# First attention: masks of the scores moved from TensorE products to GpSimd, key blocks weighed in pairs

## What is computed

```python
bias = slopes[None, :, None, None] * pos_diff[None, None, :, :]
causal = jnp.where(jnp.triu(jnp.ones((s, s), bool), 1), -jnp.inf, 0.0)[None, None]
s0 = jnp.einsum('bhqd,bhkd->bhqk', q0, k0) * scale - bias + causal
s1 = jnp.einsum('bhqd,bhkd->bhqk', q1, k1) * scale - bias + causal
w0 = jax.nn.softmax(s0, axis=-1)
w1 = jax.nn.softmax(s1, axis=-1)
...
diff_weights = w0 - lamb * w1
heads = jnp.einsum('bhqk,bhkd->bhqd', diff_weights, v).transpose(0, 2, 1, 3)
```

## Time and profile before

| | us |
|---|---|
| three runs, lowest / median / highest | 4068.45 / 4080.18 / 4084.04 |
| span of the profiled execution | 4082.1 |
| busy in it: PE / DVE / ACT / POOL | 3563.8 / 2450.6 / 2022.2 / 1270.3 |

### The profile page before, as it was taken

How to read it: one execution, slowest core, us unless ns; L and a number is a source line. 1 busy time by engine, 2 the same in 40 slices (tenths; PEclk the granted TensorE clock), 3 DMA queues, 4 the chain that set the end, 5 groups by cost and what they waited for, 6 DMA issues and landing times. The chain is left out here.

```text
span 4082.1 us, 86911 instructions
## 1 busy us (share of the span) xinstructions
PE 3563.8 (87%) x28212; PEld 2170.8 (53%) x28212; DVE 2450.6 (60%) x5697; ACT 2022.2 (50%) x3970; POOL 1270.3 (31%) x1812
## 2 busy tenths in 40 slices
PE   5799999969996698995999986788986699999997
PEld 2344444436774222222677762368974366666665
DVE  5677777741113688885677776517646566666654
ACT  5466666643335477773233334333344565656562
POOL 0111111100001011110677762605565344444440
PEclk9799999979997799996999997887788799999999
DMA  4322222200001311110666631130005233333330
GB/s 125 83 56 55 57 53 59 48 1 16 11 6 42 79 45 43 41 36 12 174 159 157 160 94 60 36 101 3 3 18 71 86 118 114 118 114 114 118 105 21
DMA packets 198052, 287.18 MB, mean 70 GB/s; under 512 B 40922, under 2 KB 155297, under 8 KB 197461
## 3 DMA queue, kind: packets, MB, share of 16 engines
q1 hardware_dynamic: 193688, 275.28, 24.2%
q0 software_dynamic: 4096, 8.40, 1.4%
HBM read 232.38 MB, written 35.84 MB: 66 GB/s over the span
## 5 line engine op out<-in xcount | busy, mean ns | idle before, releaser
L709 ACT ACTIVATE att_E<-att_pX,att_gs 128x512 f32<-128x512 f32 (+3 forms) x1024 | 723.5, 740 | 421.2 <-PE att_pX L643 176.5
L742 DVE TENSOR_REDUCE att_mx<-att_pS 128x1 f32<-128x512 f32 (+4 forms) x960 | 732.4, 787 | 202.7 <-PE att_pS L617 170.5
L1833 POOL TENSOR_TENSOR att_E<-att_E,att_rz 128x128 f32<-128x128 f32 (+3 forms) x512 | 358.3, 721 | 430.9 <-DVE att_rz L2041 430.9
L637 PE MATMUL att_pX<-arr_qs,arr_ks 75*128 75x512 bf16 (+4 forms) x1536 | 427.3, 334 | 27.6 <-ACT att_E L709 12.6
L612 PE MATMUL att_pS<-arr_ks,arr_qs 72*128 72x512 bf16 (+4 forms) x1536 | 410.3, 339 | 42.9 <-DVE att_pO L732 12.6
L1573 POOL TENSOR_TENSOR pairs_h<-pairs_m,pairs_r 128x512 f32<-128x512 f32 x272 | 346.4, 1274 | 192.0 <-DVE pairs_m L1636 182.9
L574 POOL CAST att_mp<-att_m 16x128 bf16<-16x128 f32 x288 | 81.2, 282 | 932.9 <-DVE att_m L753 907.7
L1597 PEld LDWEIGHTS pairs_po<-pairs_a,pairs_h 128*128 128x128 f32 x2176 | 286.4, 192 | 130.2 <-issue 129.4
L654 PE MATMUL att_pO<-att_E,att_vs 128*9 128x512 f32 (+3 forms) x3072 | 328.6, 500 | 1.3 <-ACT att_E L709 1.3
L1618 ACT ACTIVATE pairs_r<-pairs_ph 128x512 f32<-128x512 f32 x272 | 162.6, 598 | 327.6 <-PE pairs_ph L1589 327.6
L1972 ACT ACTIVATE att_E<-att_S,att_nm 128x128 f32<-128x128 f32 (+3 forms) x512 | 282.1, 556 | 38.6 <-DVE att_nm L2035 38.5
(11 more groups left out here) (411 smaller groups left out, 6551.5 us busy)
## 6 DMA issues: line engine op xcount, KB each, us to landing
pairs_c<-weights SPq DMA_DIRECT2D x272, 256.0 KB, 3.9
att_bias<-in_bias_dram SPq DMA_DIRECT2D x64, 896.0 KB, 4.5
parts<-proj_part SPq DMA_DIRECT2D x144, 128.0 KB, 2.3
att_xb<-xnT SPq DMA_DIRECT2D x64, 256.0 KB, 2.7
arr_qs<-parts SPq DMA_DIRECT2D x192, 64.0 KB
arr_ks<-parts SPq DMA_DIRECT2D x192, 64.0 KB
att_w<-in_w3a_dram SPq DMA_DIRECT2D x64, 192.0 KB, 2.4
arr_qs<-parts SPq DMA_DIRECT2D x96, 96.0 KB
```

What stands on the lines that cost most here:

```text
L637: ins = nc.tensor.matmul(dst[:, n], ks[:, g % NB, x, kt * P:(kt + 1) * P], qs[:, g % NB, x, q0(kt):], start=(apart or n == 0), stop=not ca ...
L709: nc.scalar.activation(E[:, kt % 2, WIDE * xp:WIDE * (xp + 1), :w], places(c)[0], ACT.Exp, scale=gs[:, g % 2, gain_of:gain_of + 1]).then_i ...
L742: V.reduce_max(dst, src, AX.X).then_inc(s_mx, 1)
L1833: nc.gpsimd.tensor_tensor(E[:, k, :width(j)], E[:, k, :width(j)], rz[:, u, k:k + 1].broadcast_to([P, width(j)]), ALU.mult).then_inc(s_n, 1)
```

## The change

All of it is in att0 and in tables made for it; the second attention keeps its order.

- The mask products L641 and L643 of the scores are gone. Their place is taken by `cut` on POOL: after the exponential of a score step, an `affine_select` in place sets the later keys in the diagonal block to zero (two units, 128 columns each). Eight per group, each waiting for ACT (`s_e`), and counted by the new semaphore `s_cut`, for which `weigh` now waits.
- So that the exponential of a later key stays finite, 48 rows are added to the product (`STEPS0`): each has an edge in the sequence and adds -1e30 where the query is before it and the key is not. Only pairs between two edges, some ten positions apart, come to the exponential unmasked. The rows per score product grow from 79 to 127.
- The key blocks are weighed in pairs: 0 and 1 at s = 5, 2 and 3 at s = 1 of the next group. `E` gets four buffers. ACT copies `pO` at step 2 instead of 1.
- POOL: cuts 0 and 1, the split of the next group's maxima, cuts 2 to 4, gains and values of the next group, cuts 5 to 7.
- The masks of the maxima (L617) stay products: `BY_DVE` is 4, and every cell has j below 4. The branch of `extreme` that adds a mask table on DVE is not reached; its table (`later`) is loaded, and waited for once.

```diff
+STEPS0 = 48
...
-        K2 = STACK + self.NX + 3
+        K2 = STACK + self.NX + 3 + self.NS
...
-            sp.dma_start(dst[STACK:, :].rearrange("r b x t -> r (b x) t"), self.ext[:, k:k + 1].broadcast_to([self.NX + 3, self.NB * self.UN, T])).then_inc(self.s_ce, 16)
+            sp.dma_start(dst[STACK:, :].rearrange("r b x t -> r (b x) t"), self.ext[:, k:k + 1].broadcast_to([self.NX + 3 + self.NS, self.NB * self.UN, T])).then_inc(self.s_ce, 16)
...
+            sp.dma_start(self.later[:, :], self.later_of).then_inc(self.s_lt, 16)
...
+        BY_DVE = 4
...
+    SLOTS = QT if causal else 2
...
-        E = p.sb("E", [P, 2, UN, T])
+        E = p.sb("E", [P, SLOTS, UN, T])
...
+                def values(at, i, g, early):
+                    if not early:
+                        pool.wait_ge(s_pv, of(at, QT, g - 2, QT))
+                    n = bass.ds((i * NB + g) * GH, GH)
+                    nc.gpsimd.tensor_copy(gs[:, g % 2], gains[:, n])
+                    nc.gpsimd.tensor_copy(vs[:, g % 2], vtok[:, n, :, :]).then_inc(s_vs, 1)
+
+                def cut(at, g, c):
+                    kt, xp = divmod(c, PER)
+                    own = E[:, kt, WIDE * xp:WIDE * (xp + 1), :P]
+                    pool.wait_ge(s_e, of(at, NP2, g, c + 1))
+                    pool.nop(nofuse=True)
+                    nc.gpsimd.affine_select(own, own, [[0, WIDE], [1, P]], ALU.is_ge, 0.0, base=0, channel_multiplier=-1).then_inc(s_cut, 1)
...
+                        for c in range(NP2):
+                            cut(at, g, c)
+                            if c == 1 and more:
+                                split(at, g + 1, first and g + 1 < 2)
+                            if c == 4 and more:
+                                values(at, i, g + 1, first and g + 1 < 2)
...
-                    if causal and apart:
-                        for n in range(2):
-                            ins = nc.tensor.matmul(dst[:, n, :P], mb[:, 2], mb[:, 1], start=False, stop=True, skip_group_check=True)
-                    elif causal:
-                        ins = nc.tensor.matmul(dst[:, :, :P], mb[:, 2], mb[:, 1:2].broadcast_to([P, 2, P]), start=False, stop=True, skip_group_check=True)
...
-                    pe.wait_ge(s_e, of(at, NP2, g, PER * (kt + 1)))
+                    pe.wait_ge(s_cut if causal else s_e, of(at, NP2, g, PER * (kt + 1)))
...
+                            if causal and s == 1 and not (first and g == 0):
+                                weigh(at, g - 1, 2, False)
+                                weigh(at, g - 1, 3, False)
+                            if causal and s == 5:
+                                weigh(at, g, 0, first and g == 0)
+                                weigh(at, g, 1, first and g == 0)
...
-                    if xp == 0 and not (first and g == 0 and kt < 2):
-                        act.wait_ge(s_pv, of(at, QT, g, kt - 1))
+                    if xp == 0 and not (first and g == 0 and kt < SLOTS):
+                        act.wait_ge(s_pv, of(at, QT, g, kt - SLOTS + 1))
...
-                            if s == PER // 2 and not (first and g == 0):
+                            if s == (2 if causal else PER // 2) and not (first and g == 0):
```

More of the change, by code:

```diff
@@ L275, with __init__ @@
     UN, NB = 4, 4
-    def __init__(self, p, maps, parts, ext, gain, masks=None):
+    def __init__(self, p, maps, parts, ext, gain, masks=None, later=None):
         self.GH = self.UN // maps
         self.NX = 0 if masks is None else 4
+        self.NS = 0 if masks is None else STEPS0
         self.NL = 2 * len(RUNS) * 16
-        self.parts, self.ext, self.gain, self.masks = parts, ext, gain, masks
-        K2 = STACK + self.NX + 3
+        self.parts, self.ext, self.gain, self.masks, self.later_of = parts, ext, gain, masks, later
+        K2 = STACK + self.NX + 3 + self.NS
         self.qs = p.sb("qs", [K2, self.NB, self.UN, T], BF16)
@@ L286, in __init__ @@
         self.mb = None if masks is None else p.sb("mb", [P, 3, P], BF16)
-        self.s_c, self.s_ce, self.s_mk = p.sem("c"), p.sem("ce"), p.sem("mk")
+        self.later = None if masks is None else p.sb("later", [P, T])
+        self.s_c, self.s_ce, self.s_mk, self.s_lt = p.sem("c"), p.sem("ce"), p.sem("mk"), p.sem("lt")
         self.s_in = [p.sem(f"in{u}") for u in range(self.NB)]
@@ L518, in attend_phase @@
         s_m0 = p.sem("m0")
+        s_cut = p.sem("cut")
         COUNT = NG // NB
@@ L584, in body @@
                         split(at, 0, True)
+                        if causal:
+                            values(at, i, 0, True)
                     for g in range(NB):
-                        if not (first and g < 2):
-                            pool.wait_ge(s_pv, of(at, QT, g - 2, QT))
-                        n = bass.ds((i * NB + g) * GH, GH)
-                        nc.gpsimd.tensor_copy(gs[:, g % 2], gains[:, n])
-                        nc.gpsimd.tensor_copy(vs[:, g % 2], vtok[:, n, :, :]).then_inc(s_vs, 1)
-                        if not (last and g + 1 >= NB):
-                            split(at, g + 1, first and g + 1 < 2)
+                        more = not (last and g + 1 >= NB)
+                        if not causal:
+                            values(at, i, g, first and g < 2)
+                            if more:
+                                split(at, g + 1, first and g + 1 < 2)
+                            continue
+                        for c in range(NP2):
+                            cut(at, g, c)
+                            if c == 1 and more:
+                                split(at, g + 1, first and g + 1 < 2)
+                            if c == 4 and more:
+                                values(at, i, g + 1, first and g + 1 < 2)
                 run_bodies(pool, COUNT, body)
@@ L609, in pass1 @@
                     w = w1(j)
+                    masked = causal and j < BY_DVE
                     for n, x in enumerate(xs):
@@ L685, in body @@
                                 turn_maxima(at, g + 1, first)
-                            if s == 0 and not (first and g == 0):
+                            if causal and s == 1 and not (first and g == 0):
[4 more added lines that the diff above has]
+                                weigh(at, g, 1, first and g == 0)
+                            if not causal and s == 0 and not (first and g == 0):
                                 weigh(at, g - 1, QT - 1, False)
-                            if s % PER == 0 and s:
+                            if not causal and s % PER == 0 and s:
                                 weigh(at, g, s // PER - 1, first and g == 0)
@@ L736, in extreme @@
                     dve.wait_ge(s_p1, of(at, NP1, h, c + 1))
+                    if causal and j >= BY_DVE:
+                        k, w = xs[0] * QT + j, w1(j)
+                        dve.wait_ge(s_mx, of(at, NP1, h, c - 1))
+                        dve.nop(nofuse=True)
+                        V.tensor_tensor_reduce(out=seen[:, c % 2, :w], in0=pS[:, bank, :w], in1=arr.later[:, T - w:], scale=1.0, scalar=-3.0e38,
+                                               op0=ALU.add, op1=ALU.max, accum_out=mx[:, h % NB, k:k + 1]).then_inc(s_mx, 1)
+                        return
                     src = pS[:, bank, :len(xs) * w1(j)].rearrange("p (n w) -> p n w", n=len(xs))
@@ L3338, in layout @@
     hi, lo8 = pos // 256 * 256, pos % 256
-    t["ext0"] = f(np.stack([[one, one, -hi, -lo8] + [0 * one] * 3, [hi, lo8, one, one] + [one] * 3]).transpose(1, 0, 2).astype(np.float32))
+    edge = (np.arange(1, STEPS0 + 1) * T // (STEPS0 + 1))[:, None]
+    early, late = np.where(pos[None] < edge, -1e30, 0.0), np.where(pos[None] >= edge, 1.0, 0.0)
+    t["ext0"] = f(np.stack([[one, one, -hi, -lo8] + [0 * one] * 3 + list(early), [hi, lo8, one, one] + [one] * 3 + list(late)]).transpose(1, 0, 2).astype(np.float32))
     t["ext1"] = f(np.stack([np.zeros((3, T)), np.ones((3, T))]).transpose(1, 0, 2).astype(np.float32))
```

24 lines of the change are left out of this document (15 added, 9 removed).

## The result

The changed kernel takes 4040.3 us (median of four runs, 4030.8 to 4050.1), the kernel before 4076.7 us in the runs beside it (four, 4068.5 to 4084.0). The ratio is 0.991, interval 0.989 to 0.993: faster by 0.9%. The forecast was 4047 in a range of 4024 to 4150, with faster as the likeliest case. The profiled execution of after has a span of 4039.9 us (4082.1 before).

A forecast was written before the change was run, and what follows sets the result against it. PE and DVE bound the first attention's groups by turns: 3.30 + 6.83 = 10.13, taken as 10.2 us against 10.81. Over 62 groups 37.8 us saved, less 4.5 once per run, gave 4047 us, range 4024 to 4150.

The forecast's parts named there:

- First stretch: Cell 9 to cell 2 of the maxima, DVE's chain: 3.30 us forecast, 0.72 less than 4.02.
- Second stretch: Cell 2 to the next cell 9, where PE is the slow one: 6.83 us forecast against 6.79 before.
- five masks: Score steps 2 to 6, second stretch: removed mask products save 0.11 us each, 0.55 us in all.
- stops at cells 3, 6, 9: PE's stops for DVE maxima in the second stretch vanish behind longer PE work: 0.8 us saved.
- weighings: Blocks 2 and 3 move from the first stretch to the second, behind cell 2: 0.89 us added there.
- transposes: Transposes of the results, formerly right behind block 1, need a switch of their own: about 0.1 us added.
- cell 5: With no weighing between cells 3 and 7, cell 5 waits for DVE to finish cell 3: 0.4 us added.
- Price of a cut: GpSimd's AFFINE_SELECT: 0.65 us plus 0.1 for wait and issue; bounded above by the power row, 1.204 us (128 x 4).
- second rival: POOL becomes the bound, at 0.925 us per cut with issue: time from 4080 us up; chance 0.25.
- The 0.2 us to spare for the maxima: Split and DMA of the maxima ready 7.3 us after cell 2; PE reaches their score step at 7.5.
- Once per run: Costs outside the groups: 2 + 1 us for constant loads at the start, 1.5 us in the last group.
- The pairs give back: Rival: hand-overs at cells 3 to 8 undo the masks' gain, group 10.7 us, about 4078 us; chance 0.20.

The follow-up runs named there:

- a1: The changed kernel with masks gone but weighings back at their old places and no cuts: 4071.7 us, group 10.57 us.
- d2: d1 with each part of the maxima signalled by its own cast and sent at once: 4021.9 us, group 9.78 us.
- f1: d2 with DVE's negation of the maxima moved behind cell 0, from behind cell 2: 4021.2 us, group 9.78 us.
- a2: The changed kernel with the scores' mask products kept on PE, weighings in pairs, no cuts: 4066.5 us, group 10.35 us.
- a4: The changed kernel with each cut on GpSimd done twice, a drain between: 4051.9 us, group 10.28 us.
- a5: The changed kernel with each cut done three times, a drain of GpSimd between: 4332.1 us, group 14.75 us.
- a3: The changed kernel without the cuts on GpSimd, weighings waiting for ACT: 4044.9 us, group 10.04 us.
- d1: The changed kernel with block 2 weighed at s = 0 ahead of the maxima's turn, block 3 alone at s = 1: 4019.2 us.
- c1: The changed kernel with the constant rows of qs and ks loaded in eight pieces through the first projection: 4038.2 us.
- f2: f1 with key block 1 weighed at s = 6 behind cell 9, not paired with block 0: 3992.5 us, group 9.40 us.
- g1: c1, d2, f1 and f2 together, unused table not loaded: 4000.5 us (five runs), ratio 0.981 to the kernel before.
- h1: The changed kernel with mask products of score steps 0, 1 and 7 put back beside the cuts: 4041.5 us.

## Why the prediction was right

**What bounds the kernel.** Right: PE and DVE take turns, and the distances between starts tell it, not PE's busy share. a1 and d2, which took work from PE in its slow stretch, ran into waits for DVE; f1, which moved DVE's, gained nothing.

**First stretch.** Forecast 3.30 us, measured 3.39. Cell 2 is released by DVE (487.78) with no weighing ahead, as it should be.

**Second stretch.** Forecast 6.83, measured 6.52. The terms of the sum can be read one by one, from start to start, with these rows of before beside the timeline of after:

```profile
485.56 0.28 PE L641 MATMUL att_pX<-arr_mb 128*128 128x128 bf16 x2
...
488.04 0.38 PE L612 MATMUL att_pS<-arr_ks,arr_qs 76*128 76x512 bf16 x1
...
488.54 0.27 PE L643 MATMUL att_pX<-arr_mb 128*128 128x256 bf16 x1
...
490.77 0.33 PE L612 MATMUL att_pS<-arr_ks,arr_qs 76*128 76x384 bf16 x1
...
491.38 0.27 PE L643 MATMUL att_pX<-arr_mb 128*128 128x256 bf16 x1
```

| term, us | forecast | measured | read from |
|---|---|---|---|
| five masks | -0.55 | -0.55 | 0.11 each; in a2 each of the five adds 0.10 to 0.11 between the same cells, on the mean of the groups |
| stops at cells 3, 6, 9 | -0.8 | -0.79 | from the mask ahead to the cell, less 0.11: 0.28, 0.20 and 0.31 in before, none in after |
| weighings | +0.89 | +0.65 | 0.97 + 0.76 in before; 1.62 (482.78 to 484.40) + 0.76 (488.44 to 489.20) in after |
| transposes | +0.1 | -0.06 | 0.50 (490.27 to 490.77) in before, 0.44 (491.45 to 491.89) in after |
| cell 5 | +0.4 | +0.39 | cell 4 to cell 5: 0.23 (487.81 to 488.04) in before, 0.62 in after |
| cell 8 | none | +0.09 | cell 7 to cell 8: 0.22 in before, 0.31 in after |

The measured terms add up to -0.27, and 6.79 less 0.27 is 6.52. So two terms were too large: the weighings, which the sum took at their price apart where in pairs they are cheaper, and the switch for the transposes, which no run shows. One was left out, the short wait at cell 8. 0.24 and 0.16 less 0.09 are the 0.31 us. The terms for the masks, the stops and cell 5 came out as worked out. The 10.13 us of the sum were then rounded up to 10.2, where this group has 9.91.

**Price of a cut.** The mis-sized term: 0.65 + 0.1 us against 0.40, and 0.37 from start to start where three follow each other (1.11 for three at 481.90). The nearest row by size was a better guide than the power row, and still 60% too high. The Trainium skill's rule for loops with branching (GPSIMD Engine Reference, section 3.1, Elementwise), an estimate of 2.56 us, is six times the measured price: the trace does not agree with it for this instruction, and the measurement decides. As the cuts were off the path, the miss moved nothing but POOL's share (50 for 85%), and that gap is the reason why the second rival did not come: its mechanism and its point are real (a4, a5), its condition was not met.

**What waits on the cuts.** The weighing's load waits up to 0.3 us for POOL, 27.1 us in 580, a little over the 0.2 that the prediction allowed, and a3 shows that it costs the groups nothing. The split kept its place (2.04 us behind cell 2, from 487.79 to 489.83, where the sum had 2.06). The 0.2 us to spare for the maxima were 0.14 (3.14 against 3.0), and d1 shows how near that was.

**Once per run.** 3 us for the start were too little: 5.5 by the trace, most of it the constants' by c1. The 1.5 us for the end are there, but for the most part not by what the sum named. From the last negation to `out_hT` it is 27.15 us in before (819.0 to 846.1) and 28.49 in after (777.4 to 805.9), 1.3 more, and there PE waits for the maxima of the last group, where the earlier trace rows had 0.16 us:

```profile
783.91 0.60 PE L667 MATMUL att_pX<-arr_qs,arr_ks 127*128 127x512 bf16 x2 [1.29 <-DMA arr_qs<-att_mp]
```

In d2, f1 and f2, whose parts are sent one by one, the end takes 27.0 to 27.1 us, with the last cut ahead of the weighing all the same (g1, with 28.7, has no wait for that DMA either); a3, without cuts, has 27.6 with a wait of 0.96. The stage adds up: from the first negation to the last 47.1 us are saved, less 5.6 at the start and 1.3 at the end is 40.2. Against the forecast the groups gave some 8 us more, and start and end took 2 more.

**The rivals.** "The pairs give back" was not the outcome, but it names the next limit: its DVE that runs dry stands at cell 9 (0.98 us), not in hand-overs at cells 4 to 8, and is worth 0.38 us once d2 has cleared the rest.

**Open.** One group of after takes 12.73 us: PE waits 2.04 us for a maxima DMA that is late.

```profile
274.34 0.65 PE L667 MATMUL att_pX<-arr_qs,arr_ks 127*128 127x512 bf16 x2 [2.04 <-DMA arr_qs<-att_mp]
```

Such groups come in one or two places of after, a3, c1, h1 and d1, the longest with waits for that DMA of 1.5 to 2.0 us, and in none where the parts are sent one by one, nor in before, a1, a2 and a4. a5's late groups are of another kind, with no wait for that DMA. What delays the DMA was not shown.

## What to carry to other kernels

Where two engines hand work to each other, price an edit by the stretch in which it stands: three of eight like products cost nothing, the other five on the mean two thirds of their own price, since waits behind them took the rest back, and which is which could be read from the timeline beforehand. Work put together in blocks is cheaper for its own engine, but look at what the other engine does meanwhile; the pair that let DVE run dry saved 0.11 us of PE, and parting it brought 0.38. An engine that only has spare time is a good place for masks, and the point from which it would bind can be worked out and then found by doing the work twice.

## What the runs showed of the hardware

- `affine_select` on GpSimd, 128 x 256 f32 in place: 0.40 us, 0.37 from one to the next, less than the TENSOR_TENSOR of the same size (0.648).
- POOL binds at 77% of records where two of three instructions of 0.4 us are followed by a drain (a5, with 28.0 of 580 us of waits for ACT). A drain between two cuts leaves 0.13 us idle, and the second starts 0.54 us behind the first, not 0.37 (a4).
- Two weighings in a row cost PE 0.11 to 0.13 us less than apart: 1.62 us against 0.97 + 0.76, and 0.76 against 0.34 + 0.55.
- A score product of 127 rows takes what one of 79 took: in h1, which has a mask behind it as before, 0.43 us from the products of a step to its mask, the same as 482.44 to 482.87 in the earlier trace rows:

```profile
483.68 0.60 PE L667 MATMUL att_pX<-arr_qs,arr_ks 127*128 127x512 bf16 x2
...
484.11 0.28 PE L671 MATMUL att_pX<-arr_mb 128*128 128x128 bf16 x2
```
